# Moving the layer-norm arithmetic of a six-layer block from GpSimd to VectorE and ScalarE

## What is computed

```python
for i in range(6):
    xn = _adaln(x, noise_emb, n1_w[i], n1_b[i])         # norm 1
    q, k, v = jnp.split(xn @ qkv_w[i].T, 3, axis=-1)     # 16 heads of 8, rope on q and k
    x = x + _attn(q, k, v, src_mask).reshape(B, L, D) @ so_w[i].T
    xn = _adaln(x, noise_emb, n2_w[i], n2_b[i])         # norm 2
    x = x + _attn(rope(xn @ cq_w[i].T), rope(context @ ck_w[i].T), context @ cv_w[i].T, ctx_mask) @ co_w[i].T
    xn = _adaln(x, noise_emb, n3_w[i], n3_b[i])         # norm 3
    x = x + (gelu(xn @ f1_w[i].T + f1_b[i]) @ f2_w[i].T + f2_b[i])

def _ln(x, eps=1e-05):
    m = jnp.mean(x, axis=-1, keepdims=True)
    v = jnp.var(x, axis=-1, keepdims=True)
    return (x - m) * jax.lax.rsqrt(v + eps)
```

## Time and profile before

| | us |
|---|---|
| median of three runs | 3133.25 (3123.37 to 3134.01) |
| the profiled execution, its time | 3124.97 |
| its span in the profile | 3123.2 |
| TensorE busy in it | 2484.5 (80%) |
| VectorE busy | 1574.3 (50%) |
| ScalarE busy | 1114.5 (36%) |
| GpSimd busy | 359.4 (12%) |
| mean granted clock of TensorE | 0.82 of full |

### The profile page before, as it was taken

One profiled execution on the slowest core, in us unless ns is written; L12 is line 12 of the kernel. 1 busy time (PEld: TensorE's weight loads), 2 busy tenths in 40 slices (PEclk: granted clock), 3 DMA queues, 4 the chain that ended last, 5 costly groups with the idle time before them and its releaser, 6 DMA issues. The chain is left out here.

```text
span 3123.2 us, 31029 instructions
## 1 busy us (share of the span) xinstructions
PE 2484.5 (80%) x10964; PEld 950.8 (30%) x10964; DVE 1574.3 (50%) x3161; ACT 1114.5 (36%) x1840; POOL 359.4 (12%) x723
## 2 busy tenths in 40 slices
PE   5999797499985947888787878878788887865599
PEld 3333233233332412222223222222322222222244
DVE  2666756446664346535455454545445454521544
ACT  0333232022221314363444536344363634432121
POOL 0000000011101040120201112020111202001000
PEclk9999888699996977686877769677786968775799
DMA  2000000200000020000100000010000000001000
GB/s 107 1 1 1 1 1 11 99 1 1 1 1 1 0 80 1 21 21 1 35 1 21 15 21 22 1 35 1 21 15 21 21 1 21 1 1 64 21 1 7
DMA packets 37946, 54.26 MB, mean 17 GB/s; under 512 B 5121, under 2 KB 34594, under 8 KB 36258
## 3 DMA queue, kind: packets, MB, share of 16 engines
q1 hardware_dynamic: 37794, 52.28, 5.2%
HBM read 32.34 MB, written 0.52 MB: 11 GB/s over the span
## 5 line engine op out<-in xcount | busy, mean ns | idle before, releaser
L2033 DVE TENSOR_REDUCE C_nm<-ps 128x1 f32<-128x512 f32 x768 | 491.3, 684 | 385.8 <-PE ps L1480 376.7
L1890 ACT ACTIVATE C_prob<-ps 128x512 f32<-128x512 f32 x768 | 415.5, 593 | 317.5 <-PE ps L1501 294.3
L1480 PE MATMUL ps<-C_ks,C_qs 62*128 62x512 bf16 x768 | 253.6, 500 | 102.9 <-DVE C_nm L2033 84.6
L1501 PE MATMUL ps<-C_qs,C_ks 64*128 64x512 bf16 x768 | 213.9, 444 | 50.1 <-ACT C_prob L1890 41.5
L1516 PE MATMUL ps<-C_prob,C_va 128*32 128x512 f32 x1536 | 235.6, 695 | 0.2
L102 POOL TENSOR_TENSOR lnt<-rs 128x4 f32<-128x4 f32 x108 | 21.4, 198 | 1287.0 <-DVEq L2027 1281.3
L1480 PEld LDWEIGHTS ps<-C_ks,C_qs 62*128 62x128 bf16 x768 | 50.7, 97 | 365.8 <-DVE C_nm L2033 234.0
L1597 PE MATMUL ps<-C_kc,C_qx 32*128 32x308 f32 x384 | 122.3, 726 | 29.4 <-DVE C_nmx L2088 13.1
L1934 ACT ACTIVATE C_u<-ps,C_biasx 77x512 f32<-77x512 f32 x192 | 120.8, 678 | 68.3 <-PE ps L1624 61.7
L1620 PE MATMUL ps<-C_qx,C_kc 32*77 32x512 f32 x384 | 128.9, 750 | 20.5 <-ACT C_u L1934 11.7
L633 DVE TENSOR_REDUCE A_nm<-ps 128x2 f32<-128x1024 f32 x64 | 77.6, 1212 | 115.4 <-PE ps L416 115.3
(11 more groups left out here) (374 smaller groups left out, 4096.7 us busy)
## 6 DMA issues: line engine op xcount, KB each, us to landing
C_qs<-C_parts SPq DMA_DIRECT2D x72, 128.0 KB, 2.4
C_ks<-C_parts SPq DMA_DIRECT2D x72, 128.0 KB, 2.3
C_w<-in_C_w SPq DMA_DIRECT2D x6, 1090.0 KB, 5.0
D_w<-in_D_ew SPq DMA_DIRECT2D x8, 768.0 KB, 10.0
B_w<-in_B_ew SPq DMA_DIRECT2D x8, 514.0 KB, 9.5
normw<-in_norm_w SPq DMA_DIRECT2D x1, 2688.0 KB
A_w<-in_A_w SPq DMA_DIRECT2D x2, 1024.0 KB, 9.7
A_w<-in_A_w SPq DMA_DIRECT2D x2, 768.0 KB, 7.9
```

What stands on the lines that cost most here:

```text
L1480: pe.matmul(ps[:, S_BANK + hp, :], lhsT=qs[side(hp, MAX_ROW), b, 2 * q + pq, t * P:(t + 1) * P], rhs=ks[side(hp, MAX_ROW), b, 2 * q + pq, ...
L1501: pe.matmul(ps[:, ST_BANK + hp, :], lhsT=ks[side(hp, HALF), b, 2 * q + pq, kt * P:(kt + 1) * P], rhs=qs[side(hp, HALF), b, 2 * q + pq, :], ...
L1890: act.activation(prob[:, kt % 2, pq, hp, :], ps[:, ST_BANK + hp, :], ACT.Exp, scale=SCALE)\
L2033: dve.tensor_reduce(nm[:, q % 2, t, pq, hp:hp + 1], ps[:, S_BANK + hp, :], AX.X, ALU.max, negate=True).then_inc(max_done, 1)
```

## The change

On VectorE `seed` becomes the complete `rstd_steps`: after the three seed instructions it runs three Newton rounds of three instructions (L79 to L81), and one more instruction writes -mean * inverse root into `m.lnu`. This last one signals `seeded`. On ScalarE a new `apply` waits for `seeded` and issues four activations of 128 x 128, Identity with a scale (the inverse root) and a bias (-mean * inverse root) of one value a partition, from `m.y` into `m.xn`; the last signals `xn_ready`. It stands in the same slots as GpSimd's `apply` did: 3, 27 and 32. `newton_steps` and GpSimd's `apply` are gone, with their semaphore. TensorE's and SP's orders are as before.

```diff
@@ GpSimd
-                def apply(n, count):
-                    pool.wait_ge(seeded, count)
-                    newton_steps(cp, pool, m, TB)
-                    for t in range(TB):
-                        k = n % B * TB + t
-                        ins = pool.tensor_scalar(m.xn[:, k, :], m.y[:, k, :], m.mv[:, t, 0:1], m.rs[:, t:t + 1],
-                                                 ALU.subtract, ALU.mult)
-                        if t < TB - 1:
-                            cp.step(ins)
-                    ins.then_inc(xn_ready, 1)
...
@@ ScalarE
+                def apply(n, count):
+                    act.wait_ge(seeded, count)
+                    for t in range(TB):
+                        k = n % B * TB + t
+                        ins = act.activation(m.xn[:, k, :], m.y[:, k, :], ACT.Identity, bias=m.lnu[:, t:t + 1],
+                                             scale=m.rs[:, t:t + 1])
+                    ins.then_inc(xn_ready, 1)
...
+                    if s == C_NORM2:
+                        apply(c, norms(c, 1))
...
+                    if s == C_NORM3:
+                        apply(c, norms(c, 2))
...
+                    if s == C_NORM1:
+                        apply(n, norms(n, 0))
@@ VectorE
                 def seed():
-                    seed_steps(c_, dve, m, TB, False)
-                    dve.sem_inc(seeded, 1)
+                    rstd_steps(c_, dve, m, TB, False)
+                    dve.scalar_tensor_tensor(m.lnu[:, 0:TB], m.mv[:, 0:TB, 0], -1.0, m.rs[:, 0:TB], ALU.mult, ALU.mult)\
+                        .then_inc(seeded, 1)
```

More of the change, by code:

```diff
@@ L95, in seed_steps @@
     c.after(dve.tensor_scalar(y.bitcast(I32), t.bitcast(I32), -1.0, float(RSQRT_MAGIC), ALU.mult, ALU.add))
[L98 to L105, removed]
 def norm_steps(c, dve, m, src, dst, n, rms=False, row=None, apart=None):
@@ L1422, in stage_c @@
          q_sum, k_sum, parts_ready, q_rem, k_rem, q_p3, k_p3, stacked, va_ready,
-         bias_added, seeded, order_p, cross_loaded, kc_ready, sel_made) = \
+         bias_added, seeded, cross_loaded, kc_ready, sel_made) = \
             (m.sem("C_" + n) for n in
@@ L1429, in stage_c @@
               "parts_ready", "q_rem", "k_rem", "q_p3", "k_p3", "stacked", "va_ready",
-              "bias_added", "seeded", "order_p", "cross_loaded", "kc_ready",
+              "bias_added", "seeded", "cross_loaded", "kc_ready",
               "sel_made"))
@@ L1814, in _ @@
                     pool.memset(one[:], 0.0).then_inc(consts_set, 1)
-                cp = Chain(pool, order_p)
-                def apply(n, count):
-                    pool.wait_ge(seeded, count)
-                    newton_steps(cp, pool, m, TB)
-                    for t in range(TB):
-                        k = n % B * TB + t
-                        ins = pool.tensor_scalar(m.xn[:, k, :], m.y[:, k, :], m.mv[:, t, 0:1], m.rs[:, t:t + 1],
-                                                 ALU.subtract, ALU.mult)
-                        if t < TB - 1:
-                            cp.step(ins)
-                    ins.then_inc(xn_ready, 1)
                 def begin(n, s):
-                    if s == C_NORM1:
-                        apply(n, norms(n, 0))
                     if s == C_K:
@@ L1845, in rest @@
                     b = c % B
-                    if s == C_NORM2:
-                        apply(c, norms(c, 1))
                     if s == C_HT2:
@@ L1853, in rest @@
                             .then_inc(vx_ready, 1)
-                    if s == C_NORM3:
-                        apply(c, norms(c, 2))
                     if s == C_HT3:
@@ L1861, in rest @@
                             .then_inc(bias_added, 1)
-                begin(0, C_NORM1)
                 for one in (qs, ks):
@@ L1982, in _ @@
                 act.wait_ge(consts_made, CONSTS_MADE)
-                for s in range(C_HT1, C_SPLIT2 + 1):
+                for s in range(C_NORM1, C_SPLIT2 + 1):
                     begin(0, s)
```

## The result

The changed kernel takes 3229.85 us (median; 3218.57 to 3234.40) against 3133.63 for the kernel before, a ratio of 1.031 (95% interval 1.027 to 1.034). I had forecast the side, slower, but 53 us of it (3186, range 3145 to 3212); it is 96. The profiled execution took 3218.57 us, 93.6 more than the profiled one before.

What follows compares the result with a forecast made beforehand. The prediction put GpSimd's Newton steps and scaling on the path of TensorE's transposes, with other queues close behind. Its terms, -6 - 13 + 10 + 34 + 33 = +58 us, led to 3186 us, with an 8-in-10 range of 3145 to 3212.

Steps and rivals of the forecast that it cites:

- the bound and the new chain: GpSimd's Newton steps and scaling are on the path; seed to transposes, alone, takes 3.7 us in place of 6.7.
- the last unit: At its two norms, where TensorE idles anyway, the shorter chain gains 3.0 us each, -6.0 us.
- norm 2: In 11 turns the wait for row maxima replaces that for `xn`; 1.2 us gained each, -13 us.
- norm 3: In 11 turns activations delay the turned-maxima copy and its stacking DMAs; +0.9 us each, +10 us.
- norm 1: In 11 turns ScalarE waits for `seeded` ahead of tile 21's exponentials, delaying TensorE; +3.1 us each, +34 us.
- the scaling on VectorE: Four scalings there take 1.07 us against 1.6 on ScalarE: 0.5 us quicker, but 1.07 more ahead of row maxima.
- The four delay terms: Queue effects at the norms, with the last unit: -6, -13, +10 and +34 us, +25 without the clock falling.
- the clock term: TensorE's clock falls around norm 1's longer pause: +3.0 us a turn, times 11 = +33 us.
- Stalls without the clock falling: Rival: norm 1 holds its clock despite the pause; sum +25 us, 3150 to 3158; chance 0.12.
- The two cancel: Rival: norm 1 costs 1 us, norm 3 nothing, no clock fall; -8 us, 3115 to 3140; chance 0.10.
- The low clock stays longer: Rival: 5 us more at the low level behind norm 1, 25 us in all; 3208 to 3216; chance 0.10.
- The waits go and nothing takes their place: Rival: ScalarE's queue has room at norms 3 and 1; 41 us gained, 3084 to 3092; chance 0.08.

Runs made afterwards that it cites:

- e1: The kernel before with only norm 1 going the new way (Newton on VectorE, activations on ScalarE), norms 2 and 3 as before: 3192.29 us.
- e4: The changed kernel with the four activations later in ScalarE's queue, at norm 3 behind the maxima copy, at norm 1 in slot 35: 3145.35 us.
- e12: ScalarE's part alone against the kernel before: scaling on ScalarE in the changed kernel's slots, Newton rounds kept on GpSimd: 3203.42 us.
- e8: VectorE's part alone against the kernel before: Newton rounds on VectorE, scaling kept on GpSimd, ScalarE untouched: 3104.11 us.
- e7: e4 with six idle copies on VectorE, 1.2 us a turn, ahead of norm 2's Newton rounds: 3061.84 us.
- e9: The changed kernel with four idle copies on VectorE, 0.8 us a turn, ahead of norm 3's Newton rounds: 3256.75 us.
- e5: The changed kernel with four idle copies on VectorE, 0.8 us a turn, ahead of norm 2's Newton rounds: 3160.08 us.
- e6: The changed kernel with eight idle copies on VectorE, 1.6 us a turn, ahead of norm 2's Newton rounds: 3184.00 us.

## Why the prediction was right or wrong, point by point

- **Right: the bound and the new chain.** Ten VectorE instructions were priced at 2.0 us; from the seed's end (2161.56) to L2011's (2163.53) they took 1.97. Four activations were priced at 1.6 between 1.15 and 1.84; they take 1.65, 481 ns each:

```profile
L1882 ACT ACTIVATE xn<-y,lnu,rs 128x128 f32<-128x128 f32 x144 | 59.2, 481 | 248.3 <-DVE lnu L2011 217.0 <-DVEq L2164 31.3
```

- **Right: the last unit.** 3.0 us each at two norms, as worked out (9.36 to 6.36 us of idle time).
- **Right: norm 2.** Bound by the row maxima; -1.2 forecast, -1.55 measured. The maxima start 1.89 us behind the seed's end (2163.45) and not 0.14, so they are held back by 1.75 us and not by the 2.0 of the sum.
- **Right: norm 3.** The DMA behind the delayed copy is last, as named; +0.9 forecast, +0.4 measured, since L1491 to the transposes is 0.54 us and not 0.93.
- **Right in mechanism, small in size: norm 1.** +3.1 forecast, +4.2 measured. The stall was priced right: the copy of the turned maxima ended 5.1 us after the seed's end, and I had 5.3. The missing 1.1 us is mostly the low clock inside the wait: the weighing of the values (L1506) takes 1.93 us where it took 1.07 at full clock, and tile 24's scores (2276.56) follow right behind it, without a wait for the stacking DMAs that I had named for this place. e1, e4 and e12 confirm that ScalarE's place in its queue is what costs.
- **Not tested: the scaling on VectorE.** By the rule of the Trainium skill (ScalarE: Activation LUTs, Rules for kernel authors), additions and multiplications belong on VectorE. No run puts the scaling there; in e8, 126 us faster than the changed kernel, it is on GpSimd.
- **The four delay terms and the last unit** summed to +25 us; measured they are +27, with 12 us of clock inside norm 1's. That the two agree so well is in part luck: norm 1's term came out 12 us above its forecast, norm 2's 4 us and norm 3's 6 us below theirs.
- **Wrong: the clock term**, +33 us. Its condition, "if the low level lasts 10.3 us here too", came true: the clock does fall at norm 1, in the 11 us from the seed it is 0.72, 6.2 us at the low level,

```profile
2268.00:2279.00 11.00, 6.19 (x25) 1.16 (x21) 1.70 (x11) 6.58 (x14) 0.00 (x0) 0.72 0.00 1
```

  and in the 10 us behind the transposes another 4.1 (clock 0.80). The step that failed is to take this for all that the clock would do: "the least is 0, the most 10.3 x 0.45 = 4.6", with nothing for the rest of a turn. Next to norm 1 the clock costs 1.1 us inside the wait, where I had 0.3, and the piece behind the transposes is 0.6 us longer, where I had 2.7: some 19 us in all and not 33. That piece holds as much low clock as before (153 us in 11 turns, 152 before); more of it comes early and less late. The larger cost is some 45 to 120 us further on, in the stretch behind norm 2: +62 us, where I had nothing. I had taken the clock as something that a pause does to the work next to it. The runs show it act on the whole turn: the same 312 records take 69, 73, 77 or 78 us, and a delay anywhere can move all turns from one group to another. The price for each us at the low level, 0.45, was right (0.46); the number of us was not: the changed block has 178 us more of them than the old one, not 113. No range that took only local effects could hold this. A fair width can be read from the runs: the time less the kernel before beside it and less the measured delays and idle copies lies between -40 us (e7) and +87 (e9), and is +70 for the changed kernel. The kernel before was near the good end, with seven of eleven stretches of the shortest kind. A turn became 9.3 us longer in the mean of ten (146.1 against 136.9, from norm 2 to norm 2), and not 5 to 6.
- **The rivals.** "Stalls without the clock falling" (3150 to 3158) did not happen here. Its time is nearly e5's, 3160, but that is luck, since e5's clock falls at norm 1 as well (5.8 us at the low level in the wait). "The two cancel" did not happen: norm 1 cost 4.2 us and not 1. "The low clock stays longer" was the right direction for a wrong reason, and too small. "The waits go and nothing takes their place" (3084 to 3092) is what e8 does at the norms, without ScalarE; it took 3104, with 39 us more behind norm 2.

What stays open: by which rule the clock's changes fall where they do, and so why 0.8 us ahead of norm 2 brings the shortest stretches and 0.8 us ahead of norm 3 the longest. The runs show the groups and the shift between them; they don't show what picks one. How often another execution of the same kernel falls into other groups isn't shown either, as one was profiled of each; e4's ten took 3128 to 3158 us. A kernel that keeps TensorE busy through the pauses wasn't tried.

## What to carry to other kernels

An engine with a third of its time free can still be the wrong place: look at what stands behind the new wait in its queue, and who waits for that; here four cheap activations in front of two exponentials and one small copy cost 4.2 us a turn, and three slots later nothing. When a kernel repeats a turn and TensorE's clock changes in it, cut the trace into pieces with the same instructions and compare the same piece over the turns and the kernels before crediting an edit with it. Before judging such an edit, time it with a little idle time added here and there: e5 against the changed kernel shows that 70 us can belong to the alignment and not to the edit.

## What the runs showed of the hardware that I had not expected

- Idle time made a kernel faster: 0.8 us more a turn, 70 us less in all (3229.85 to 3160.08), and 1.2 us more a turn, 84 us less (3145.35 to 3061.84). The same 0.8 us at another place cost 27 us (3256.75).
- The low clock can hold through busy work: 44.0 us at 1.2 GHz with TensorE busy for 41.6 of them, while the same 312 records in a neighbouring turn had 18 us less of the low level in all.
- Turns settle. In e4, e5, e7 and e9 every one of the eleven stretches is of the same kind, and in e1 and e6 two kinds alternate. e4 and e5 repeat turns of 139.95 us, equal to a tenth of a us, though their norms and idle copies differ by 7 us a turn.
